# A fused metaformer kernel: row gathers that start in the merge, and two of four gates spread by TensorE

## The reference

```python
x = x + conv(ln_c(x))            # s = relu(xn^T xn)^2, out = g s, with g = Wc xf + bc
t = to_tokens(x); v = ln_t(t)
h = (v_flat @ W_gat).reshape(M, 4, 4)
src, dst = edges + one loop per token
e = leaky_relu(a_src[src] + a_dst[dst], 0.2)
alpha = softmax of e over the edges of each dst
agg = segment_sum(h[src] * alpha, dst) + b_gat
scores = layernorm(agg).mean over heads          # 4 experts
w = softmax(top_2(scores)), 0 for the others     # the gates g[e]
t = t + sum_e g[e] * (gelu(v @ W1[e] + b1[e]) @ W2[e] + b2[e])
# edge_index = randint(0, 16 * 1024), 2 x 262144
```

## Time and profile before

| what | value |
| --- | --- |
| median of 3 runs | 5415.7 us |
| lowest and highest | 5413.36 and 5427.73 us |
| profiled execution | 5427.65 us, its span 5425.8 us |
| busy: PE, DVE, ACT, POOL | 3722.4, 3970.8, 3400.6, 2943.8 us |
| mean granted TensorE clock | 0.853 |
| moved by DMA | 441.38 MB |

### The profile page before, as it was taken

How to read it: one execution, slowest core, us unless ns; L and a number is a source line. 1 busy time by engine, 2 the same in 40 slices (tenths; PEclk the granted TensorE clock), 3 DMA queues, 4 the chain that set the end, 5 groups by cost and what they waited for, 6 DMA issues and landing times.

```text
span 5425.8 us, 61836 instructions
## 1 busy us (share of the span) xinstructions
PE 3722.4 (69%) x18367; PEld 1256.6 (23%) x18367; DVE 3970.8 (73%) x5512; ACT 3400.6 (63%) x4285; POOL 2943.8 (54%) x2937
## 2 busy tenths in 40 slices
PE   4888988300499999999999999994000017777878
PEld 1223333100133333333333333331000002222222
DVE  8998988997466666666666655555888857777877
ACT  4777888202576767676676767674555536566666
POOL 6000000007777777777777777773777137666661
PEclk9999999655699999999999999996555558888889
DMA  7000100002112222222222222223555527999997
GB/s 264 23 24 20 29 20 21 11 16 59 36 39 58 45 55 53 48 53 47 56 45 54 54 47 50 46 45 103 176 170 168 188 71 144 142 162 155 154 166 139
DMA packets 332446, 441.38 MB, mean 81 GB/s; under 512 B 183193, under 2 KB 261916, under 8 KB 331500
## 3 DMA queue, kind: packets, MB, share of 16 engines
q1 hardware_dynamic: 209744, 288.12, 19.4%
q0 software_dynamic: 105536, 148.61, 16.5%
q10 hardware_dynamic: 16896, 1.18, 0.2%
HBM read 252.35 MB, written 166.47 MB: 77 GB/s over the span
## 4 chain that ended last, share of the span: by engine, by line
POOL 36%; issue 14%; DMA 14%; DVE 8%; PE 4%; ACT 1%; SPq 1%; DVEq 0%; POOLq 0%; ACTq 0%
POOL rows L1692 33%; DMA rows<-htab_d,idx 8%; DMA gs<-gates_d 4%; PE ye L1913 2%; PE up L1925 2%; DVE ms L2594 1%; POOL R L1750 1%; DMA gates_d<-GH 1%; DVE pairs L2601 1%; ACT GT L2087 1%; DVE AD L2460 1%; DVE AE L2454 1%; POOL got L1705 0%; DVE total L2603 0%; POOL nb L1707 0%
## 5 line engine op out<-in xcount | busy, mean ns | idle before, releaser
L1692 POOL DMA_INDIRECT rows<-htab_d,idx x2048 | 2135.1, 1043 | 802.0 <-issue 595.8
L2376 DVE SCALAR_TENSOR_TENSOR s<-gram,rel 128x1024 f32<-128x1024 f32 (+1 forms) x720 | 802.7, 1117 | 860.0 <-ACT rel L2042 850.3
L2042 ACT ACTIVATE rel<-gram 128x1024 f32<-128x1024 f32 (+1 forms) x1080 | 1009.6, 940 | 605.9 <-PE gram L1860 574.5
L1818 PE MATMUL acc<-s,gT 128*64 128x512 f32 (+1 forms) x4320 | 1075.3, 576 | 0.0
L1859 PE MATMUL gram<-hl 128*128 128x512 f16 (+1 forms) x2160 | 777.1, 365 | 117.9 <-DVE s L2376 93.1
L1860 PE MATMUL gram<-hl,lh 128*128 128x512 f16 (+1 forms) x2160 | 765.8, 360 | 0.0
L1750 POOL DMA_INDIRECT R<-seg_d,nidx x576 | 588.5, 1022 | 191.4 <-issue 165.8
L1913 PE MATMUL ye<-hid,w 128*64 128x384 f32 x1536 | 376.1, 569 | 273.0 <-DVE ms L2594 208.6
L1030 POOL IOTA slots<- 64x2048 int32 x1 | 1.8, 1833 | 975.4 <-POOLq L182 975.4
L2134 ACT ACTIVATE hid<-up,b1t 128x768 f32<-128x768 f32 x384 | 333.3, 899 | 269.3 <-PE up L1925 267.9
L1896 PE MATMUL tailsT<-ident,tails 128*20 128x128 f32 x24 | 5.3, 414 | 652.1 <-DVE tails L2482 652.1
(11 more groups left out here) (372 smaller groups left out, 5349.8 us busy)
## 6 DMA issues: line engine op xcount, KB each, us to landing
gs<-gates_d SPq DMA_DIRECT2D x64, 1024.0 KB
rows<-htab_d,idx POOLq DMA_INDIRECT x2048
seg_d<-state SPq DMA_DIRECT2D x32, 996.0 KB, 4.3
raw_d<-w_zeros POOLq DMA_DIRECT2D x48, 512.0 KB, 22.5
raw_d<-rows POOLq DMA_DIRECT2D x32, 768.0 KB, 3.6
tne<-tn_d SPq DMA_DIRECT2D x32, 576.0 KB, 6.6
x2e<-x_d SPq DMA_DIRECT2D x32, 576.0 KB, 9.8
out<-res SPq DMA_DIRECT2D x64, 256.0 KB
```

The lines of the kernel that those rows point to most:

```text
L1692: pool.indirect_dma_start(out=n.rows[:, k % 2, j, :], out_offset=None, in_=n.htabx, in_offset=bass.IndirectOffsetOnAxis(ap=n.idx[:, g % 2, ...
L1818: last = pe.matmul(acc[(par + c) % 2][j * C:(j + 1) * C, 0:w], gT[:, par, 2 * k + j, :], s2[:, u % SLOTS, j * w:(j + 1) * w], start=k == 0 ...
L2042: act.activation(rel[:, t % RELS, 0:2 * w].rearrange("p (j x) -> p j x", j=2), gram[(par + t) % 2][:, :, 0:w], ACT.Relu, scale=1.0 / SPLIT ...
L2376: dve.scalar_tensor_tensor(halves(s2[:, t % SLOTS, 0:2 * w]), gram[(par + t) % 2][:, :, 0:w], 1.0 / SPLIT ** 2, halves(rel[:, t % RELS, 0: ...
```

## The change

The merge and the flow become one block. `merge_nodes` no longer runs its parts itself but hands them to `flow`, whose engine programs call them first. With that:
- **Gathers.** POOL's gather code moves to module level. SP loads the first indices right behind the store of `gidx_d`; the first 48 gathers (OPENING) are issued in the merge, behind a new count v_need, and the rest up to AHEAD x 64 follow without a break. AHEAD goes from 28 to 31. `need` has 32 counts in place of 8, and one is read at each chunk of 64.
- **Segments.** `a_ends` is raised behind AE, and a new `a_got` behind GT. DVE waits for `a_got` only ahead of the first operation that reads GT; POOL's reuse of the buffers waits for `a_got`.
- **Gates.** Experts 0 and 1 keep the old path. The gates of experts 2 and 3 are split into three bf16 parts, stored as `parts_d`, loaded as 12 short rows (`gk`), and multiplied by a 0/1 matrix `pick` on PE (`spread_gates`, once per chunk) into a PSUM tensor that takes the place of the third `up` buffer (UPS = 2). ACT copies it to `gs2`.

```diff
+IN_FLIGHT = 4
+EARLY = 10
+OPENING = 48
...
-    n.gates = nc.dram_tensor("gates_d", (NX, M), F32).ap()
+    n.NW = NX // 2
+    n.gates = nc.dram_tensor("gates_d", (n.NW, M), F32).ap()
+    n.parts = nc.dram_tensor("parts_d", (3 * (NX - n.NW), M), BF16).ap()
...
+def gather_rows(pool, n, t0, t1):
+    GC, G, NK = n.GC, n.G, 4 * n.G
+    for t in range(t0, t1):
+        k, j = divmod(t, GC)
+        g, c = divmod(k, 4)
+        if j == 0:
+            need = pool.value_load(n.need[0:1, NK - 1 - k:NK - k], min_val=16, max_val=16 * n.B)
+            pool.wait_ge(n.o_hx, need)
...
-        block = ctx.enter_context(nc.Block())
...
+            sp.wait_ge(ids_out, 16)
+            for par in range(2):
+                sp.dma_start(n.idx[:, par, :, :], ids_of(n)[n.G - 1 - par]).then_inc(n.i_in[par], 16)
...
             pool.wait_ge(one_out, 16)
-
-        @block.tensor
-        def _(pe):
+            pool.wait_ge(v_need, 1)
+            gather_rows(pool, n, 0, OPENING)
...
-    AHEAD = 28
+    AHEAD = 31
...
-        up = [late.enter_context(nc.psum_tensor(f"up{i}", [P, 2, 512], F32)) for i in range(GROUP)]
+        up = [late.enter_context(nc.psum_tensor(f"up{i}", [P, 2, 512], F32)) for i in range(UPS)]
+        gp = late.enter_context(nc.psum_tensor("spread", [P, 2, 512], F32))
...
+            def spread_gates(b, par, nth, cp):
+
+                if cp == 0:
+                    pe.wait_ge(gl_in[par], 128 * (nth + 1))
+                at_least(pe, a_gs, b * ECH + cp)
+                for k in range(NL):
+                    last = pe.matmul(gp[:, k, 0:EW], pick[:, k, :], gk[:, par, cp * EW:(cp + 1) * EW], start=True, stop=True)
+                last.then_inc(pe_gs, 1)
...
-                    if before or i >= GROUP:
-                        pe.wait_ge(a_hid, b * ESTEPS + i + 1 - GROUP)
+                    if before or i >= UPS:
+                        pe.wait_ge(a_hid, b * ESTEPS + i + 1 - UPS)
...
+                    if k == 1:
+                        spread_gates(b, par, nth, cp)
...
-                act.activation(AE[:, par, :, :], nb[:, par, :, HE + NH:HE + 2 * NH].rearrange("p j h -> p h j"), ACT.Copy)
-                act.activation(GT[:, par, :, :], got[:, par, ::-1, 0:HE + NH].rearrange("p j w -> p w j"), ACT.Copy).then_inc(a_ends, 1)
+                act.activation(AE[:, par, :, :], nb[:, par, :, HE + NH:HE + 2 * NH].rearrange("p j h -> p h j"), ACT.Copy).then_inc(a_ends, 1)
+                act.activation(GT[:, par, :, :], got[:, par, ::-1, 0:HE + NH].rearrange("p j w -> p w j"), ACT.Copy).then_inc(a_got, 1)
...
+                    if i % NX == 1:
+                        cp = i // NX
+                        act.wait_ge(pe_gs, b * ECH + cp + 1)
+                        if before or cp >= 2:
+                            act.wait_ge(v_m, (b * ECH + cp - 1) * NX)
+                        act.activation(gs2[:, (par + cp) % 2, :, :], gp[:, :, 0:EW], ACT.Copy).then_inc(a_gs, 1)
...
+                    link(dve.tensor_tensor(gx[:, :, :], U1[:, :, NW:NX], half4, ALU.mult))
...
+                    link(dve.tensor_copy(upper, gx[:, :, :]))
+                    link(dve.tensor_tensor(gx[:, :, :], gx[:, :, :], upper, ALU.subtract))
+                    link(dve.tensor_copy(middle, gx[:, :, :]))
+                    dve.tensor_tensor(lower, gx[:, :, :], middle, ALU.subtract).then_inc(v_gt, 1)
```

More of the change, by code:

```diff
@@ L111, in kernel_program @@
         n.o_hx = sem("o_hx")
+        n.i_in = [sem("i_in0"), sem("i_in1")]
+        n.j_in = [sem("j_in0"), sem("j_in1")]
+        n.landed = [sem(f"landed{f}") for f in range(IN_FLIGHT)]
+        n.raw_out = [sem("raw_out0"), sem("raw_out1")]
+        n.opened = sem("opened")
         n.o_tn = sem("o_tn")
@@ L941, in _, with store_rows, ids_of @@
                 s += 1
+def store_rows(pool, n, k):
+    chunk = n.raw[n.CW:n.E + n.CW, :].rearrange("(k p j) c -> k p (j c)", p=P, j=n.GC)
+    end = (k + 1) * n.GC
+    for f in range(IN_FLIGHT):
+        pool.wait_ge(n.landed[f], 16 * ((end - f + IN_FLIGHT - 1) // IN_FLIGHT))
+    pool.dma_start(chunk[4 * n.G - 1 - k], n.rows[:, k % 2, :, :].rearrange("p j c -> p (j c)")).then_inc(n.raw_out[k % 2], 16)
+def gather_rows(pool, n, t0, t1):
[6 more added lines that the diff above has]
+            pool.wait_ge(n.o_hx, need)
+            pool.sem_inc(n.opened, 1)
+        if j == 0 and c == 0:
+            if g < 2:
+                pool.wait_ge(n.i_in[g], 16)
+            else:
+                pool.wait_ge(n.j_in[g % 2], 16 * (g // 2))
+        if j == 0 and k >= 2:
+            pool.wait_ge(n.raw_out[k % 2], 16 * (k // 2))
+        if t >= IN_FLIGHT:
+            pool.wait_ge(n.landed[t % IN_FLIGHT], 16 * (t // IN_FLIGHT))
+        pool.indirect_dma_start(out=n.rows[:, k % 2, j, :], out_offset=None, in_=n.htabx,
+                                in_offset=bass.IndirectOffsetOnAxis(ap=n.idx[:, g % 2, 3 - c, j:j + 1], axis=0)).then_inc(n.landed[t % IN_FLIGHT], 16)
+        if j == EARLY - 1 and k:
+            store_rows(pool, n, k - 1)
+            if c == 0 and 1 <= g < G - 1:
+                pool.dma_start(n.idx[:, (g + 1) % 2, :, :], ids_of(n)[G - 2 - g]).then_inc(n.j_in[(g + 1) % 2], 16)
+        if t == NK * GC - 1:
+            store_rows(pool, n, NK - 1)
+def ids_of(n):
+    return n.gidx.rearrange("(q c p j) a -> q p c (j a)", c=4, p=P, j=n.GC)
 def merge_nodes(nc, n):
@@ L1344, in flow @@
         xs = ph("xs", [P, TW, NX])
-        GH = ph("GH", [P, 2, NX, TW])
+        GH = ph("GH", [P, 2, NW, TW])
+        GB = ph("GB", [P, 2, 3 * NL, TW], BF16)
+        gx = ph("gx", [P, TW, NL])
+        picki = ph("picki", [6 * NL, 2], I32)
+        pickf = ph("pickf", [6 * NL, 2])
+        side = ph("side", [6 * NL, NL, 2])
+        pick = ph("pick", [6 * NL, NL, P], BF16)
         tne = ph("tne", [P, 2, HALF])
@@ L1400, in flow @@
         x_out = sem("x_out")
-        passed = sem("passed")
-        sp_passed = sem("sp_passed")
-        landed = [sem(f"landed{f}") for f in range(IN_FLIGHT)]
-        raw_out = [sem("raw_out0"), sem("raw_out1")]
         img_done = sem("img_done")
@@ L1544, in _ @@
             sp.dma_start(groups(ml), in_rows(n.mkey, 0)).then_inc(k_in, 16)
-            for par in range(2):
-                sp.dma_start(n.idx[:, par, :, :], gid[G - 1 - par]).then_inc(i_in[par], 16)
             sp.wait_ge(v_q, 1)
@@ L1709, in _ @@
             t = AHEAD * GC
-            gather(0, t)
+            gather_rows(pool, n, OPENING, t)
             pool.wait_ge(img_done, 1)
+            pool.iota(picki[:, :], pattern=[[0, 2]], base=0, channel_multiplier=1).then_inc(n.c_rdy, 1)
             for k in range(NK):
@@ L2433, in _ @@
             by_row = lambda t: t.rearrange("p h j -> p j h")
+            dve.wait_ge(n.c_rdy, 5)
+            link(dve.tensor_scalar(pickf[:, 1:2], picki[:, 1:2], 3.0 * NL, None, ALU.is_ge))
+            link(dve.tensor_scalar(picki[:, 0:1], picki[:, 0:1], NL - 1, None, ALU.bitwise_and))
+            link(dve.tensor_copy(pickf[:, 0:1], picki[:, 0:1]))
+            for k in range(NL):
+                link(dve.tensor_scalar(side[:, k, 1:2], pickf[:, 0:1], float(k), None, ALU.is_equal))
+                link(dve.tensor_tensor(side[:, k, 0:1], side[:, k, 1:2], pickf[:, 1:2], ALU.is_gt))
+                link(dve.tensor_tensor(side[:, k, 1:2], side[:, k, 1:2], pickf[:, 1:2], ALU.mult))
+            link(dve.tensor_copy(pick[:, :, :].rearrange("r k (h c) -> r k h c", h=2), side[:, :, :].unsqueeze(3).to_broadcast([6 * NL, NL, 2, C])))
+            dve.sem_inc(v_set, 1)
             lanes = lambda t: t.rearrange("p h j -> p (h j)")
```

133 lines of the change are left out of this document (61 added, 72 removed).

## The result

| | before | changed |
|---|---|---|
| median of 5 runs each, us | 5420.9 (5413.4 to 5427.7) | 5452.9 (5444.2 to 5459.2) |
| ratio | | 1.0058, 95% interval [1.0047, 1.007] |
| span of the profiled execution, us | 5425.8 | 5451.1 |

The account below looks back on a forecast made before the run. It took PE to bound the images, a full POOL to leave 66 us of slack before the segments, and DMA to be busiest in the combine stage. Terms +106, -49 and +6 made +63 us on median 5415.7: 5479, range 5402 to 5545.

Parts of the forecast that it names:

- First `got`: POOL's first fetch of segment rows: at 3835 us instead of 3729, as more gathers go ahead; +106 us.
- the strict reading: Gathers beside DVE's merge: descriptor writing is left alone, so 90 fit instead of the 60 taken, 38 us better.
- Segment stage: First `got` to last scan: fewer steps with gathers and split semaphores, 612 us instead of 661.3; -49 us.
- Combine stage: Stage storing the results: waits and last load give -62 us, new gate work costs +68; sum +6.
- The waits and the last load: Combine stage, gate loads with half the bytes: all DVE waits for `gs` go, -55 us; last load halves, -7.
- The new work: Combine stage, gate work added on PE, DVE and ACT: 2.2 us an image, +68 us over 31 images.
- No DVE wait for `gs`: Combine stage, sign to look for: DVE no longer waits for gate loads, where it waited 55.0 us.
- Stores 29 us apart: Combine stage, sign to look for: the stores of results come 29 us apart.
- Rival 3: Combine stage: the gates' chain is late again, now at PE; +138 us, 5554 us; chance 0.07.
- Rival 1: Combine stage: transfers are its bound, not occasional waits; sum -86 us, 5330 us; chance 0.1.
- Rival 2: Gathers' lead near its bound (+18 to +40), gate work only 0.8 us (-37); 5397 to 5419 us; chance 0.15.
- Rival 4: Start of gathers: they do not start before the merge ends, index loads landing late; 5554 us; chance 0.02.

Follow-up runs that it names:

- experiment 1: The changed kernel with AHEAD set back from 31 to 28; ratio 0.9975 to the kernel before.
- experiment 2: The changed kernel with AHEAD 30 instead of 31; ratio 0.9945 to the kernel before.
- experiment 5: The changed kernel with POOL waiting for the end of DVE's merge of edges before its first gather; ratio 1.0172 to the kernel before.
- experiment 4: The kernel before with only the semaphores split, AE and GT announced by two instead of one; ratio 0.9973.
- experiment 3: The changed kernel with AHEAD 29 and PIECE 8 (gathers a step) instead of 31 and 11; ratio 0.9922 to the kernel before.
- experiment 6: Four runs on the changed kernel's gates: without spreading 1.0068; that with half the gate bytes 0.9988; that with two `up` buffers 1.0056; without spreading matmuls and copies 1.0057.
- experiment 7: The changed kernel with AHEAD 29, PIECE 8 and the `gk` loads on their own semaphore, so PE skips the large gate load; ratio 0.9897 to the kernel before.

## Why the prediction was right, and where its terms were off

It said 5479 us with a range of 5402 to 5545, and slower; the kernel took 5452.9. On the profiled execution the sum was +63 us, and +25 came out; by the medians it was 32. The sign and the mechanism of the loss were right, the size was twice too large: 25 us too much on the first `got`, 6 on the segments, 7 on the combine stage.

- **First `got`: +106 forecast, +81 measured**, within the bounds of +70 and +121. The mechanism was right, as experiments 1, 2 and 5 show. The term was mis-sized in two places. The count stood at 1869 at 3663.1 and not at 1852. I let a gather beside the long DVE operations miss every second boundary, 2.3 us each, and take 1.5 us beside the short ones. The trace has two gathers in three long operations, 1.77 us each, and 1.3 us beside the short ones, so 71 fitted in and not 60, and 6 more were won among the images, which I had at no change. These 17 gathers are 21 us. Of the 7 us for reading counts 2 or 3 appeared (115 gathers at 1.27 us in place of 1.25); the first gather came 2.7 us later than I said.
- **The rule of the Trainium skill.** The Trainium skill, SBUF — State Buffer, section "Who interferes with whom", says that a DVE instruction with two SBUF inputs contends with a GpSimd instruction that reads SBUF. A gather reads its indices `idx` there, so this sentence does not speak for the 90 gathers of the strict reading; those rested on a remark of the page that is marked as inferred, that writing descriptors needs the write side only. The trace has 71, and beside the 1.22 us operations the long gathers end 0.8 us behind a boundary of DVE's: the contention is real there, and only smaller than the rows at 1266 us made it.
- **Segment stage: 612 us forecast, 606.8 measured.** Six steps of 20.3 were right to the tenth. The others took 18.42 and not 18.5, and the first scan came 24.2 us behind the first `got` and not 27.6. The split of the semaphore did what I said where I said it (experiment 4). Gathers and segments together were to cost +57 us (+18 to +93) and cost +26.
- **What I didn't ask** is whether the larger lead is needed for the gain. I held PIECE fixed; with 8 in place of 11 the steps are quick with the gathers in them (experiment 3). The rows gave only half of the answer: 11 gathers of 1.25 us and two fetches are 16 us, which would have fitted under DVE's step; that steps with 11 took 20.33 us said that something on POOL took longer. It is the gather held by DVE's scan.
- **Combine stage: +6 forecast, -1 measured (+3.1 up to its first store, -4.4 from there), but by two errors that cancel, which is luck.** The waits and the last load were to give 62 us; half the bytes alone gave 45 of the stage (experiment 6), since other waits moved in. The 7 us of the last load did not come: the last image took 20.0 us before, 20.4 without spreading, 19.9 with half the bytes and 21.3 in the changed kernel. The new work was to cost 2.2 us per image and costs 1.2: PE's matmuls and ACT's copies, which I had at 0.9 and as part of 0.4, cost 0.21 together; DVE's operations 0.55 and not 0.9; the third buffer 0.44, which was the whole of the 0.4 that I gave to both. The work itself was not overrated: the six matmuls take 1.3 us an image in the trace (1.4 forecast, of which no row shown gave the 0.4 us for changes of type), ACT's three copies 2.4 (2.7), and DVE's five new operations, less what GH shrank by, 1.16 (0.9). What was wrong is how much of it stays uncovered. "No DVE wait for `gs`" held. "Stores 29 us apart" held (28.6).
- **Rival 3** (the gates late at PE) was there in a small form: 13.3 us in the changed kernel, 31 to 37 in experiments 1 to 3 and 5. No lengthening of the stage by it could be measured (experiment 7), so the price of 55 us and the clock behind it was too high. **Rival 1** (transfers bound the images) is out: half the bytes left the quickest images where they were. **Rival 2** (+18 to +40 for gathers and segments, -37 for the gates) was right on the lead, where +26 came out and not the +57 of the forecast, and wrong on the gates: the new work costs 1.2 us and not 0.8, and half the bytes give less than the listed waits. The result, +25, lies between its +3 and the +63. **Rival 4** did not occur.

## What to carry to other kernels

When an engine must finish a batch of work before the next stage may open, a larger batch has to be paid for in full once that engine's slack is gone, and work that starts earlier pays back only what it adds to the batch: compare the two counts (77 won, 192 asked) before sizing anything else. Where a step alternates between two engines' bounds, look for the piece at which the other engine is still the bound; eight gathers per step were free and eleven cost 2 us, because the engine that issues them is held during a long operation of the other. Halving a transfer that is waited for now and then is worth less than the listed waits, and each operation added to the engine next to the bound is paid in every round, though not in full (0.55 us an image for 1.16 us of DVE's time).

## What the runs showed of the hardware

- Gathers beside DVE's merge settle into a fixed beat with it. Beside two-input operations of 1.22 us they take 1.97 and 0.95 us in turn, beside those of 0.69 us 0.94 to 1.02, while the same instruction alone takes 0.94. Beside the long ones a gather cost 0.5 us more than alone, half of the 1.05 us that the rows at 1266 us suggested.
- A gather that starts during DVE's scan of 3.62 us ends 0.75 to 0.77 us behind the scan's end, wherever in the scan it starts: it took 3.28 us when it started 1.09 us behind the scan's start (experiment 1), 3.70 at 0.67 (experiment 3, below) and 2.01 at 2.36 (the kernel before). So it was in all 66 scans with such a gather in these three traces. There POOL also waits up to 4.5 us for the landing of an earlier gather, yet DVE's steps stay at 18.4 to 18.6 us:

```profile
3999.46 0.98 POOL L981 DMA_INDIRECT rows<-htab_d,idx  x1 [0.30 <-issue]
...
4002.80 3.62 DVE L2536 TENSOR_TENSOR_SCAN S<-G 128x1660 f32<-128x1660 f32 x1
4003.47 3.70 POOL L981 DMA_INDIRECT rows<-htab_d,idx  x1 [3.03 <-DMA rows<-htab_d,idx]
```

- The same combine stage took from 887 to 913 us in one profiled execution each of five kernels that differ only ahead of it, while the five timed runs of the changed kernel lie within 15 us. A stage of one profile is not measured to better than some 10 us here.
